# A decoder layer on one core: the hand-ordered instruction lists, lags and PSUM banks replaced, transposes with a semaphore per buffer

## The reference

```python
# self-attention, 16 heads of 16, causal, 64 rows a sequence
q = layernorm(x) @ Wq;  k, v = layernorm(x) @ Wkv
q, k = layernorm(rotary(q * s, x)), layernorm(rotary(k * s, x))     # per head
a = softmax(causal(q @ k.T / sqrt(16))) @ v @ Wo
# second attention: 64 "channels", 256 positions, 8 heads of 8, band of 64, softmax over the band
qkv = x1.T @ w_in.T;  o = softmax(band(q @ k.T / sqrt(8))) @ v @ w_out.T
y = relu(o) * context;  out = w_ct.T @ y
# feed-forward: ternary weights, 256 -> 2 x 1024 -> 256
h = silu(x2 @ w_gate) * (x2 @ w_up);  h = rms_norm(h);  y3 = h @ w_proj
```

## Time and profile before

| | |
|---|---|
| runs | 916.16, 917.2, 924.08 us, median 917.2 |
| the profiled execution | 913.9 us, span 912.2 us |
| TensorE busy | 812.4 us, 89% |
| VectorE busy | 772.3 us, 85% |
| GpSimd busy | 698.0 us, 77% |
| ScalarE busy | 678.2 us, 74% |
| DMA moved | 57.64 MB, mean 63 GB/s |
| chain that ended last | PE 44%, DVE 16%, SP queue 13%, ACT 10%, DMA 7%, POOL 5% |
| granted TensorE clock | mean 0.965 |

### The profile page before, as it was taken

The page is one execution under the profiler, slowest core; times in us unless marked ns, Lnnn a source line. Parts: engine busy times, 40 slices in busy tenths (PEclk is TensorE's granted clock), DMA queues, the critical chain, the costliest instruction groups (busy, mean ns, idle before and its releaser), DMA issues.

```text
span 912.2 us, 23909 instructions
## 1 busy us (share of the span) xinstructions
PE 812.4 (89%) x9654; PEld 475.0 (52%) x9654; DVE 772.3 (85%) x1503; ACT 678.2 (74%) x1331; POOL 698.0 (77%) x691
## 2 busy tenths in 40 slices
PE   3788998889999999999999999999999998878865
PEld 1344544545566565555565555555556555444432
DVE  4889976868999999999999999999999988776453
ACT  1465565768888888888888888888888888665653
POOL 4498887658988898898898898898888885544521
PEclk9889997989999999999999999999999999997997
DMA  8000111211233233333333333333323324322243
GB/s 251 2 25 14 35 33 42 50 34 40 55 66 70 55 69 68 65 73 72 72 72 72 72 72 71 73 72 71 67 61 64 66 66 66 57 62 45 52 85 76
DMA packets 125030, 57.64 MB, mean 63 GB/s; under 512 B 93044, under 2 KB 124020, under 8 KB 124920
## 3 DMA queue, kind: packets, MB, share of 16 engines
q1 hardware_dynamic: 124920, 56.12, 29.3%
HBM read 13.62 MB, written 4.19 MB: 20 GB/s over the span
## 4 chain that ended last, share of the span: by engine, by line
PE 44%; DVE 16%; SPq 13%; ACT 10%; DMA 7%; POOL 5%; issue 4%; POOLq 0%; ACTq 0%; DVEq 0%
PE ps L756 7%; PE ps L558 5%; PE ps L830 4%; SPq L307 4%; PE ps L818 4%; PE ps L683 4%; ACT prob L1644 3%; DMA xin<-in_x 3%; SPq L336 3%; PE ps L596 3%; PE ps L801 2%; PE ps L609 2%; PE ps L723 2%; DMA k_rows<-qk_lo 2%; DVE rowmax L2814 2%
## 5 line engine op out<-in xcount | busy, mean ns | idle before, releaser
L2814 DVE TENSOR_REDUCE rowmax<-ps 128x4 f32<-128x768 f32 x256 | 242.6, 948 | 23.7 <-PE ps L683 22.8
L1644 ACT ACTIVATE prob<-ps 128x768 f32<-128x768 f32 x256 | 206.3, 806 | 56.6 <-PE ps L723 47.7
L2335 POOL TENSOR_TENSOR hsum<-hsum,minus_half 128x32 f32<-128x32 f32 x32 | 174.1, 5442 | 5.3 <-DVE hsum L2740 5.2
L2359 POOL TENSOR_SCALAR_AFFINE_SELECT prob<-prob 128x512 f32<-128x512 f32 (+1 forms) x128 | 114.3, 893 | 63.7 <-ACT prob L1644 63.4
L2361 POOL TENSOR_SCALAR_AFFINE_SELECT prob<-prob 128x1024 f32<-128x1024 f32 (+1 forms) x128 | 114.2, 893 | 0.0
L756 PE MATMUL ps<-prob,v_pad 128*32 128x192 f32 x2048 | 101.9, 342 | 0.0
L683 PE MATMUL ps<-k_rows,q_rows 31*128 31x192 f16 x1024 | 88.0, 250 | 15.5 <-DVE rowmax L2814 8.5
L723 PE MATMUL ps<-q_rows,k_rows 32*128 32x192 f16 x1024 | 87.4, 249 | 10.4 <-ACT prob L1644 6.8
L801 PE MATMUL ps<-wgu,xsplitT 128*128 128x512 bf16 x256 | 68.2, 391 | 16.2 <-DVE y L2849 13.5
L756 PEld LDWEIGHTS ps<-prob,v_pad 128*32 128x32 f32 x2048 | 62.0, 113 | 25.6 <-issue 10.9
L683 PEld LDWEIGHTS ps<-k_rows,q_rows 31*128 31x128 f16 x1024 | 29.6, 92 | 82.2 <-DVE rowmax L2814 35.6
(11 more groups left out here) (164 smaller groups left out, 2055.6 us busy)
## 6 DMA issues: line engine op xcount, KB each, us to landing
v_swap<-v_own SPq DMA_DIRECT2D x64, 68.0 KB, 2.2
xin<-in_x SPq DMA_DIRECT2D x32, 128.0 KB, 2.6
q_rows<-qk_hi SPq DMA_DIRECT2D x64, 64.0 KB, 2.2
k_rows<-qk_hi SPq DMA_DIRECT2D x64, 64.0 KB, 2.0
enc<-in_ctx SPq DMA_DIRECT2D x32, 128.0 KB, 2.5
out<-yout SPq DMA_DIRECT2D x32, 128.0 KB, 2.0
prob<-in_w_guT SPq DMA_DIRECT2D x4, 512.0 KB, 7.8
q_rows<-qk_lo SPq DMA_DIRECT2D x32, 64.0 KB, 2.0
```

The lines of the kernel that those rows point to most:

```text
L1644: copy(prob[:, 2 * c:2 * c + 2, :, :].rearrange("p u a b -> p u (a b)"), ps[:, STB:STB + 2, 0:2 * QW], ACT.Exp, scale=float(XD) ** -0.5).t ...
L2335: g.tensor_tensor(hsum[:, t.two, 1, :], hsum[:, t.two, 0, :], minus_half[:, :], ALU.pow).then_inc(S["head_pow3"], 1)
L2359: g.affine_select(out=lead, in_=lead, compare_op=ALU.is_ge, fill=0.0, base=BAND - 64 * kb, pattern=[[0, 8], [1, cut]], channel_multiplier=-1)
L2814: v.tensor_reduce(of_head[:, hq:hq + 2, 2 * row_of(ng):2 * row_of(ng) + 2], ps[:, MXB:MXB + 2, 0:2 * QW].rearrange("p j (a b) -> p j a b", ...
```

## The change

No computation is added or taken away: every tile goes through the same pieces, with the same shapes. What changes is in which order each engine issues them, at which lags, with which waits and in which banks.

- The order in `step(at)` of all five engines and the lags. With 2 added to the lags after (its loop counts two lower against the tiles), TensorE works on a tile's pieces at mostly the same distances; some differ (`aT_ps`, `ct_ps` and `gate_ps0` are a step nearer, `gate_ps0` now stands in the step before `gate_ps1`).
- The loop covers steps 11 to 35 instead of 11 to 37. The lists before and behind it are new. With the shift of two, the loop begins two tiles earlier and ends at `mx` of tile 28 (before, `mx` of tile 31 was started in it); `mx` of tiles 29 to 31 and `st` of 28 to 31 are written out.
- Twelve of the 20 bank constants.
- The DMA transposes `xT`, `hT0` and `hT1` signal one semaphore for each of the three buffers instead of one each for all tiles.
- `keep_warm` has other counts and places.

```diff
-FIRST_STEP, LAST_STEP = 11, 38
+FIRST_STEP, LAST_STEP = 11, 36
-XNT_B, QK_B, V_B, QKT_B, PT0_B, PT1_B, AT_B, WO_B, MAXT_B, TR_B = 6, 7, 5, 6, 7, 7, 7, 6, 6, 5
-HF_B, Z_B, CT_B, GATE0_B, GATE1_B, UP0_B, UP1_B, DOWN_B, S_B, O_B = 5, 7, 7, 5, 7, 5, 5, 7, 5, 6
+XNT_B, QK_B, V_B, QKT_B, PT0_B, PT1_B, AT_B, WO_B, MAXT_B, TR_B = 5, 7, 5, 7, 6, 6, 6, 6, 7, 7
+HF_B, Z_B, CT_B, GATE0_B, GATE1_B, UP0_B, UP1_B, DOWN_B, S_B, O_B = 6, 5, 5, 5, 5, 7, 6, 5, 5, 6
...
-        s_xT = sem("s_xT")
-        s_hT = [sem("s_hT0"), sem("s_hT1")]
+        s_xT = [sem(f"s_xT{b}") for b in range(3)]
+        s_hT0 = [sem(f"s_hT0_{b}") for b in range(3)]
+        s_hT1 = [sem(f"s_hT1_{b}") for b in range(3)]
...
             def put_xload(t):
+                if t.has(6):
+                    sp.wait_ge(S["y1"], t.back(6).at(1, 1))
                 do_xload(t)
             def put_vswap(t):
+                sp.wait_ge(S["v"], t.at(1, 1))
                 do_vswap(t)
             def put_rep_lo(t):
+                sp.wait_ge(S["qk_lo"], t.at(1, 1))
                 do_rep_lo(t)
...
             def put_pt_ps(t, c):
...
                 if c == 0:
-                    if t.has(-3):
-                        pe.wait_ge(S["qk"], t.back(-3).at(1, 1))
+                    if t.has(-1):
+                        pe.wait_ge(S["s_sub"], t.back(-1).at(1, 1))
             def put_o_ps(t):
+                if t.has(-3):
+                    pe.wait_ge(S["qk"], t.back(-3).at(1, 1))
+                pe.wait_ge(S["pt0"], t.at(1, 1))
                 pe.wait_ge(s_vswap[t.buf], t.dma(2))
-                if t.has(5):
-                    pe.wait_ge(S["zr"], t.back(5).at(1, 1))
             def put_maxT_ps(t):
-                if t.has(-6):
-                    pe.wait_ge(S["xnT"], t.back(-6).at(1, 1))
-                pe.wait_ge(S["max"], t.at(8, 8))
+                if t.has(2):
+                    pe.wait_ge(S["heads"], t.back(2).at(1, 1))
             def put_hf_ps(t):
+                if t.has(-4):
+                    pe.wait_ge(S["y1"], t.back(-4).at(1, 1))
             def put_down_ps(t):
-                if t.has(-2):
-                    pe.wait_ge(S["silu1"], t.back(-2).at(1, 1))
-                pe.wait_ge(s_hT[1], t.at(16, 16))
+                if t.has(-4):
+                    pe.wait_ge(S["zr"], t.back(-4).at(1, 1))
```

More of the change, by code:

```diff
@@ L234, in build @@
         s_maxrow = [sem(f"s_maxrow{b}") for b in range(3)]
-        s_xT = sem("s_xT")
-        s_hT = [sem("s_hT0"), sem("s_hT1")]
+        s_xT = [sem(f"s_xT{b}") for b in range(3)]
+        s_hT0 = [sem(f"s_hT0_{b}") for b in range(3)]
+        s_hT1 = [sem(f"s_hT1_{b}") for b in range(3)]
         s_vswap = [sem(f"s_vswap{b}") for b in range(3)]
[L238 to L244, removed]
+        names = """aT aT_ps attn attn_c centred centred_c ct_ps down_ps exp gate_ps0 gate_ps1 gated h_hi h_lo1 head_pow3 heads
+                   heads_c hf hf_ps hid0 hid1 hid_eps hid_pow max maxT_ps max_hi mx o_ps ot pt0 pt1 pt_ps0 pt_ps1 qk qkT qkT_ps
+                   qk_hi qk_lo qk_ps qkn rotated rotated_c s_exp s_max s_ps s_sub sel silu0 silu1 sqsum squared st tanh0 tanh1
+                   tr_ps up_ps0 up_ps1 v v_ps val variance variance_c vpad wo_ps x1 x1_nb x2 x2_hi x2_lo x2_nb x_eps x_pow x_stats
+                   x_stats_c xn xnT xnT_ps xn_nb xproj_ps y1 y1_eps y1_pow y1_stats y1_stats_c y2 y2_eps y2_pow y2_stats
+                   y2_stats_c y3 y3_eps y3_pow y3_stats y3_stats_c yout yout_nb z_ps zr"""
         S = {n: sem("c_" + n) for n in names.split()}
@@ new lines, in _ @@
+            do_xT(tile[25])
+            do_out(tile[20])
+            sp.wait_ge(S["qk_hi"], tile[30].at(1, 1))
+            do_rep_hi(tile[30])
+            sp.wait_ge(S["qk_lo"], tile[30].at(1, 1))
+            do_rep_lo(tile[30])
+            sp.wait_ge(S["max_hi"], tile[29].at(1, 1))
+            do_maxrow(tile[29])
+            do_out(tile[21])
+            do_hT(tile[24], 0)
+            do_enc(tile[29])
+            sp.wait_ge(S["x2_lo"], tile[26].at(1, 1))
+            do_xT(tile[26])
@@ L573, in put_v_ps @@
             def put_v_ps(t):
-                if t.has(1):
-                    pe.wait_ge(S["s_sub"], t.back(1).at(1, 1))
                 do_v_ps(t)
@@ L584, in put_qkT_ps @@
                 pe.wait_ge(S["qkn"], t.at(1, 1))
+                if t.has(8):
+                    pe.wait_ge(S["hid0"], t.back(8).at(1, 1))
                 do_qkT_ps(t)
@@ L643, in put_aT_ps @@
             def put_aT_ps(t):
-                if t.has(1):
-                    pe.wait_ge(S["qk_lo"], t.back(1).at(1, 1))
                 do_aT_ps(t)
@@ L770, in put_tr_ps @@
             def put_tr_ps(t):
+                if t.has(-3):
+                    pe.wait_ge(S["qk_lo"], t.back(-3).at(1, 1))
                 do_tr_ps(t)
@@ L3088, in _ @@
+            do_xn_nb(tile[4])
+            dve.wait_ge(S["o_ps"], tile[0].at(1, 1))
+            do_attn(tile[0])
+            dve.wait_ge(S["rotated"], tile[3].at(1, 1))
+            do_centred(tile[3])
             dve.wait_ge(s_x[tile[5].x_buf], tile[5].x_dma(1))
```

2950 lines of the change are left out of this document (1632 added, 1318 removed).

## The result

The kernel after takes **883.2 us** (median of 4 runs, 881.5 to 887.1), the kernel before 916.7 on the same chip (4 runs, 916.2 to 924.1). The ratio is 0.962, 95% interval 0.956 to 0.968. The profiled execution took 883.4 us, its span is 881.7. The forecast was 893, the range 875 to 912.

A forecast was written before the change was run, and what follows sets the result against it. It took SP's queue to set the 23.68 us period. From the profiled 913.9 us it took 3.6 (steady), 16 (end), 2 (last part) and 2 (head), giving 890; with 3.3 us to the median, 893 us, range 875 to 912.

The forecast's parts named there:

- What bounded before: Steady middle: the 23.68 us period is set by SP's queue, where copies that `mx` needs stand behind a waiting transpose.
- The steady part: Tiles 8 to 28: period falls to 23.5 us, 20 x 0.18 = 3.6 us gained; ends 16 gained, 12 lost.
- Rival C: POOL blocks DVE twice a tile, at `h_lo1` and `x1_nb`; period 24.3 us, total 929 us; chance 0.08.
- Rival A: `qkn` ends before `h_lo1`, so no collision; steady period 22.9 us, total 881 us; chance 0.24.
- TensorE: Steady step: its work shrinks a little to 21.9 us a tile, so it is not the bound.
- Head: Start to the steady part: fewer tiles written out, weight pieces and `keep_warm` moved; 2 us gained, ends 7 each way.
- End: First `mx` of tile 28 to first `st` of tile 31: 91 us becomes 75, 16 us gained; ends 20 and 3.
- The last part: Final 69.3 us: same five feed-forward tiles, one tile's chain bounds it; 2 us gained, ends 8 gained, 5 lost.
- At nothing: One semaphore per buffer for the transposes and new banks cost nothing by themselves.

The follow-up runs named there:

- Number 6: Kernel before, SP's queue alone changed: `xload` one tile ahead and `out`, both in front of the wait for `gated`; 900.3 us, ratio 0.984.
- number 4: Kernel after with `qkn` on POOL moved to right behind `y3_pow` of the next step; 874.4 us, ratio 0.955.
- number 2: Kernel after with `x1_nb` moved ahead of `qk` on DVE; 886.3 us, ratio 0.965 to the kernel before.
- Number 9: Kernel before with SP's written-out head of after and nine throwaway matmuls before the first `st` of tile 3; 910.4 us, ratio 0.994.
- number 10: Kernel before with five throwaway matmuls ahead of the fourth `mx` and the seventh `st` of tiles 29 to 31; 907.9 us, ratio 0.990.
- number 11: Number 4's kernel with nine throwaway matmuls in TensorE's two gaps of its last step in the loop; 868.5 us, ratio 0.946.
- number 12: Kernel after with one semaphore each for `hT0` and `hT1` again, instead of one per buffer; 888.6 us, ratio 0.967.

## Why the prediction was right, step by step

**What bounded before.** Right. SP's queue stood in the loop, and its rows are gone from the chain. Before, `mx` of tiles 10 to 25 started 0.1 to 0.5 us after the last copy had landed; in after it is 0.5 to 1.6 us, where the prediction gave 0.3 us of room. Number 6 shows it in the old kernel with nothing changed but that queue.

**The steady part, 3.6 us.** Measured 3.5, and for the stated reason: the 0.8 us that SP releases are mostly taken back by `h_lo1` under `qkn`. I had taken 0.6 us of delay between 0 and 1.4; it was 0.64, with 0.83 us of `qkn` left where I had 0.8. (The nine terms of POOL's sum add up to 19.7 us and not 19.5; the trace has 19.5, as neighbours overlap a little. Rival C's 929 us does not follow from its terms either, which give some 925; nothing hangs on it.) Rival A, 22.9 us a tile without the collision, is the measured period of number 4 to 0.05 us. In part that is luck: 22.9 was worked out as a loop over DVE with TensorE far from full, and TensorE is full there. Rival C named a double collision; the second one (`x1_nb` under `sel0`, 0.62 us) happens in every step, and costs nothing (number 2), because DVE waits behind it anyway.

**TensorE.** One statement here was wrong: that its 21.9 us a tile leave it far from the bound. It is busy 22.6 us of each period in number 4 and in number 6. With the collision gone the chain of a step runs along TensorE's own order but for `s_max` and `s_sub`, and at most 0.3 us a step are left to win from DVE. This did not enter the sum, as 23.5 is above it.

**Head, 2 us with 7 either way.** Mis-sized: 10.1, outside its own ends. The part was not worked out from the chain of that stretch, which showed 9.5 us of SP issues in a row and 17 us at the lower clock, both readable before. Number 9, with both changed, recovers 4.6 us, of which the clock could be all. The other 5.2 lie in the first three periods at full clock, 61.6 us there and 56.4 in after, so in the order of the computing engines, which was not tried alone. The counts say this much: by the first `mx` of tile 3 the old kernel had done one tile more of `head_pow3` (5.4 us of POOL), `variance`, `qk` and `qk_ps` since the first `mx` of tile 0 than the new one, and its next five periods were hardly shorter for it (114.0 us against 114.5). That this lead is what cost the time is argued, not shown.

**End, 16 us.** Measured 10.9, within the ends 20 and 3. The term that was mis-sized is the clock. Both kernels have the lower level in this stretch, 0.89 of full over 91.0 us before and 0.94 over 80.1 after, so about 20 and 10 us. In before those 20 us cost 6.2 (number 10), in number 4 the 10 cost 3.6 (number 11). Held against each other at the full clock, the old order takes 84.8 us and the new one, with `qkn` moved, 76.1: the order of the two written-out steps is worth 8.7 us. The forecast's 75 us against the same 84.8 would be 9.8, so its order was nearly right; it missed the 3.6 us of the lower level that the new order keeps. The sum of TensorE's work between marks, 70 us, was below both, as the exponentials and `sel` of the last tiles stretch it.

**The last part, 2 us.** Measured 6.0, inside its ends. No run takes it apart. In after TensorE works 41.4 us of it against 46.5, so some 5 us of its work were done sooner. It is not the clock: the lower level lasts 12.1 us in before and 12.2 in after there.

**At nothing.** The semaphores: nothing in the loop (number 12). The new banks (fourteen of the twenty constants, not twelve) and the counts of `keep_warm` were not tried alone.

**The total** came out 10 us under the forecast: head and last part gave 12 us more, the end 5 us less, and the other 3 are the step from the profiled execution to the median, which before's first runs had and these did not. The 5 us that the end fell short hid as much of the other errors: without them the forecast would have been 15 us off, with the direction and the steady part still right.
